# Value weighting ahead of the fill: the order of TensorE's work in 53 steps of an attention and feed-forward block

## What is computed

```python
# x: (1024, 256); 16 heads of 128; WINDOW = 128
h = layernorm(x)
q, k, v = split_heads(h @ wq), split_heads(h @ wk), split_heads(h @ wv)
q, k = rotary(q, cos, sin), rotary(k, cos, sin)
valid = (k_pos > q_pos - WINDOW) & (k_pos <= q_pos)
attn = softmax(where(valid, (q @ k.T) * scale, neg))
x = x + merge_heads(attn @ v) @ wo
# feed-forward, w1q and w2q rounded to -1, 0, 1 by their mean absolute value
x = x + gelu(layernorm(x) @ w1q.T + b1) @ w2q.T + b2
```

## Time and profile before

| | |
|---|---|
| median of 3 runs | 348.57 us (347.9 to 349.16) |
| the profiled execution | 347.75 us |
| its span, first to last instruction | 346.0 us |
| TensorE, matmuls | 336.5 us, 97% |
| TensorE, weight loads | 311.8 us, 90% |
| VectorE | 272.2 us, 79% |
| ScalarE | 207.7 us, 60% |
| GpSimd | 222.8 us, 64% |
| granted TensorE clock | 1.00 in every slice |

### The profile page before, as it was taken

The page is one execution under the profiler, slowest core; times in us unless marked ns, Lnnn a source line. Parts: engine busy times, 40 slices in busy tenths (PEclk is TensorE's granted clock), DMA queues, the critical chain, the costliest instruction groups (busy, mean ns, idle before and its releaser), DMA issues.

```text
span 346.0 us, 6907 instructions
## 1 busy us (share of the span) xinstructions
PE 336.5 (97%) x2398; PEld 311.8 (90%) x2398; DVE 272.2 (79%) x608; ACT 207.7 (60%) x628; POOL 222.8 (64%) x181
## 2 busy tenths in 40 slices
PE   7997999999999999999999999999999999989996
PEld 7886789999999999999999999999999999968986
DVE  5888987778777887688779998898778777878682
ACT  3355766655677677555675566556665666466280
POOL 3426896867676777667889798979767657230400
PEclk9999999999999999999999999999999999999999
DMA  6832553455553333333233333333322232000001
GB/s 212 208 97 69 146 153 93 121 149 156 133 146 99 83 79 91 94 92 93 70 87 83 83 76 94 91 94 93 91 63 61 56 83 48 0 3 0 32 30 61
DMA packets 29025, 31.25 MB, mean 90 GB/s; under 512 B 3392, under 2 KB 20288, under 8 KB 28992
## 3 DMA queue, kind: packets, MB, share of 16 engines
q1 hardware_dynamic: 28672, 30.29, 34.4%
q10 hardware_dynamic: 320, 0.52, 0.4%
HBM read 12.98 MB, written 1.05 MB: 41 GB/s over the span
## 4 chain that ended last, share of the span: by engine, by line
PE 84%; DVE 6%; POOL 4%; issue 2%; ACT 2%; DMA 1%; SPq 0%; DVEq 0%; POOLq 0%
PE PR L423 22%; PE OT L504 13%; PE VO L442 12%; PE VO L459 12%; PE SC L477 11%; PE PT L488 4%; PE PR L532 2%; PE VO L539 2%; PE SC L532 2%; POOL gT_lo L1084 1%; POOL turn L1079 1%; DMA v_raw<-in_wv 1%; PE SC L539 1%; DVE probsT L870 1%; DVE gT_lo L845 1%
## 5 line engine op out<-in xcount | busy, mean ns | idle before, releaser
L1084 POOL TENSOR_TENSOR gT_lo<-turn,gT_hi 128x512 fp32r<-128x512 f32 x61 | 80.4, 1317 | 42.9 <-ACT gT_hi L669 42.6
L1079 POOL TENSOR_TENSOR turn<-turn,swapped 128x512 f32<-128x512 f32 x61 | 78.9, 1294 | 27.8 <-DMA swapped<-by_sin 27.7
L674 ACT ACTIVATE probs<-SC,negmax 128x128 f32<-128x128 f32 x128 | 45.8, 363 | 73.6 <-DVE negmax L859 73.6
L870 DVE TENSOR_TENSOR probsT<-PT,mask_sb 128x512 f32<-128x512 f32 x64 | 44.1, 689 | 39.6 <-PE PT L488 39.6
L504 PE MATMUL OT<-probsT,v_sb 128*128 128x128 f32 x450 | 60.4, 276 | 1.4 <-DVE probsT L870 1.0
L504 PEld LDWEIGHTS OT<-probsT,v_sb 128*128 128x128 f32 x450 | 55.3, 191 | 2.7 <-DVE probsT L870 2.6
L681 ACT ACTIVATE probs<-probs,rinv 128x128 f32<-128x128 f32 x128 | 44.5, 394 | 16.6 <-DVE rinv L864 16.6
L423 PE MATMUL PR<-xT_hi,qk_lo 128*128 128x512 f32 x128 | 50.6, 395 | 0.2 <-DVE xT_lo L809 0.2
L423 PE MATMUL PR<-xT_hi,qk_hi 128*128 128x512 f32 x128 | 50.4, 394 | 0.0
L423 PE MATMUL PR<-xT_lo,qk_hi 128*128 128x512 f32 x128 | 50.3, 393 | 0.0
L669 ACT CAST gT_hi<-turn 128x512 fp32r<-128x512 f32 x64 | 38.9, 607 | 9.8 <-POOL turn L1079 7.6
(11 more groups left out here) (118 smaller groups left out, 838.9 us busy)
## 6 DMA issues: line engine op xcount, KB each, us to landing
swapped<-by_sin SPq DMA_DIRECT2D x124, 128.0 KB, 2.3
v_raw<-in_wv SPq DMA_DIRECT2D x8, 256.0 KB, 3.1
qk_raw<-in_wq SPq DMA_DIRECT2D x16, 128.0 KB, 2.5
qk_raw<-in_wk SPq DMA_DIRECT2D x16, 128.0 KB, 2.6
o_raw<-in_wo SPq DMA_DIRECT2D x8, 256.0 KB, 3.0
xres<-in_x SPq DMA_DIRECT2D x4, 256.0 KB, 4.0
w_raw<-in_w1t SPq DMA_DIRECT2D x4, 256.0 KB, 3.1
w_raw<-in_w2t SPq DMA_DIRECT2D x4, 256.0 KB, 3.2
```

The costliest lines, as they stand in the source:

```text
L674: nc.scalar.activation(probs[n % 2][:, i], SC[n % 2][:, i * 256 + P:(i + 1) * 256], ACT.Exp, bias=negmax[:, n % 2, i:i + 1], accum_out=row ...
L870: tt(probsT[:], PT[:, 0:256].rearrange("p (i q) -> p i q", i=2).unsqueeze(2).broadcast_to([P, 2, 2, P]), mask_sb[:].unsqueeze(1).broadcast ...
L1079: tt(turn[m % 4][:], turn[m % 4][:], swapped[m % 2][:], ALU.add).then_inc(rot_done, 1)
L1084: tt(rot_lo(head, c % 2)[:, half_of(c)], turn[m % 4][:], rot_hi(head, c % 2)[:, half_of(c)].bitcast(F32), ALU.subtract).then_inc(rotlo_don ...
```

## The change

In steps 8 to 60 TensorE's list has `weigh_v(n-1)` ahead of `fill(n)`. Everything else stays, the other engines' lists too; `transpose_probs(n)` stands at the head of the next step as before.

```diff
                 if n + 4 < CHUNKS:
                     project(n + 4)
-                fill(n)
-                if n == STEPS - 1:
-                    transpose_half(0)
-                weigh_v(n - 1)
+                if turned_first(n):
+                    weigh_v(n - 1)
+                    fill(n)
+                else:
+                    fill(n)
+                    if n == STEPS - 1:
+                        transpose_half(0)
+                    weigh_v(n - 1)
             ffn1(0)
```

## The result

The changed kernel takes 364.52 us (median, 364.37 to 365.03) against 348.31 us before: a ratio of 1.048, with a 95% interval of 1.045 to 1.051, and 16.2 us more. The forecast was 364.9 us. Its profiled execution has a span of 362.6 us where the one before had 346.0.

A forecast was written before the change was run, and what follows sets the result against it. TensorE, never waiting in steps 8 to 59, was taken as the bound. 11.3 + 1.4 + 4.2 = 16.9 us, less 0.6, made 16.3 and, from the 348.57 us median, 364.9 us; 8-in-10 range 359.5 to 368.5.

The forecast's parts named there:

- What bounds the kernel: Steps 8 to 59: TensorE never waits, its matmul rows cover 238.00 of 238.00 us; an added wait costs in full.
- The bank wait: Steps 8 to 59: the moved weighting waits for `ot_lo` to empty bank OT, 11.3 us in all, bounds 6.1 to 13.9.
- the two outliers: Two steps where `ot_lo` ends 0.41 and 0.38 us late behind ternary-weight work; longer steps may give back some 0.6 us.
- Rival 3: VectorE's late steps with ternary pieces reach TensorE, 2.8 us, and a handover of 0.20 adds 2.6: up to 370 us; chance 0.05.
- The second return to fp32r: Fill behind the fp32 weighting: one more change of operand type a step, 0.08 us each, 53 times, 4.2 us.
- The rival that had it free: At the fill behind the weighting, the return to fp32r costs nothing: 360.7 us; chance 0.08.
- the handover of 0.15: From the end of `ot_lo` to the weighting: a wait late by x costs x + 0.15 us, in 52 steps.
- Step 60: No projection there, so the weighting waits for `ot_lo` and the fill's hidden 1.42 us come behind: 1.4 us.
- What stays covered: Transposition's wait for `scaled` (0.63 us of cover), earlier `ot_hi`, later `copy_v` and `add_out`: no cost or gain.
- What would show it: Steps 8 to 59: some 50 OT weight-load waits of 0.1 to 0.3 us, fill spacing 0.20 then 0.12, steps of 4.9.

The follow-up runs named there:

- split fill: Changed kernel with, in steps 8 to 60, six fill products ahead of the weighting and six behind it: 348.81 us, 1.002 of the kernel before.
- run with one product ahead: Changed kernel with, in steps 8 to 60, one fill product ahead of the weighting and eleven behind it: 359.04 us, 1.032 of the kernel before.
- two products ahead: Changed kernel with, in steps 8 to 60, two fill products ahead of the weighting and the other ten behind: 352.41 us, 1.012 of the kernel before.

## Why the prediction came out

Its sum was right to 0.4 us, but two of its terms were wrong by some 3.7 us, one each way. That they cancelled was not foreseen: with either one put right alone the forecast would have missed by about 4 us.

- **What bounds the kernel: right.** TensorE had no slack in steps 8 to 59, so every wait added is paid in full. With the cover kept (split fill) it stays full, and nothing is lost.
- **The bank wait: right in place, too small in size.** The sum had 11.3 us less 0.6 for the two outliers. The outliers went, as forecast: in the changed kernel `ot_lo` ends 1.41 to 1.52 us behind the projection's first product in every step. Rival 3's late VectorE steps showed only in the run with one product ahead, once. The lateness of `ot_lo` was right too: 0.055 us a step on the mean, and 0.15 from its end to the first matmul make the 0.204 that the table shows. What was missing is 0.072 us in the weighting. The step that failed is the comparison "an unhindered weighting of eight takes 0.89 from start to start": that was read ahead of a transposition, while the hindered ones stood ahead of an fp32r product. Ahead of an fp32r product an unhindered weighting takes 0.82. So a late handover costs x + 0.22 us, and 52 x 0.276 = 14.4 us instead of 10.7.
- **The second return to fp32r: wrong.** It was priced at 4.2 us from a longer spacing. Runs with one and two returns more put it at 0.007 us a step, 0.4 us. The rival that had it free was right on this point, though its time of 360.7 was not, since it kept the handover of 0.15. A formula of the Trainium skill speaks to this, page "TensorE: Matmul & The Clock Gate", section "Back-to-back issue gap": it counts the columns alone. The section calls it the gap of an isolated matmul and says that in a stream the weight loads set the spacing too, which the prediction left out. The single rows at 0.20 us differ from the formula; the step's sum (4.560 against 4.553 us) agrees with it in having no price for what ran before.
- **The two errors are one.** The 0.07 us that a weighting seems to save ahead of an fp32r product and the 0.08 that this product seems to cost are the same overlap of rows, read once as a gain left out and once as a loss put in. That is why they are of one size.
- **Step 60: right.** 1.4 us forecast, 1.45 measured by itself.
- **What stays covered: right.** No wait of the transposition for `scaled`, of `copy_v` or of `add_out` turned up in the changed kernel, and the earlier `ot_hi` gave nothing, though ScalarE's waits for it (5.2 us) are gone.
- **What would show it: half right.** The waits are there, 52 of them, but they read 0.44 us on the mean, not 0.1 to 0.3, as they count from the end of the load before; and the profile names "issue", not the tile. Step 31, from which the 4.91 us were worked out, takes 4.88; the mean is 4.85, as 14 of the 52 weightings have six rows.

The runs give 14.4 + 0.4 + 1.4 = 16.2 us for the change. The medians differ by 16.2, the profiled spans by 16.6: 0.010 us a step, in the fill behind the weighting (1.509 against the split fill's 1.499), stay unexplained.

## What to carry to other kernels

On an engine without slack, work moved ahead of other work is safe only as far as what it waits for is done by then: compare the end of the releaser with the start of the place it moves to, step by step, and add about 0.2 us for the handover (0.22 here), since the weight load wants to be ahead of its matmul. Three small products ahead of the waiting one, 0.35 us, were enough here, while two left 0.05 us a step; splitting a filler gives freedom of order that moving it whole does not. Don't price a change of type or neighbour by the spacing of two rows alone: take the whole stretch from one group's start to the end of the next. And don't read a wait's cost from the idle time of matmul rows: of 15 us lost here they showed 2.

## What was not expected of the hardware

- An fp32 weighting takes 0.83 us from start to start ahead of a transposition and 0.75 ahead of an fp32r product (means over weightings of six and of eight rows), whose own first row is 0.36 us long instead of 0.28. The sum is the same to 0.01 us.
- A product of 256 columns behind one of 128 columns has the next start 0.17 us later instead of 0.12, with fp32r on both sides.
- A weight load that comes up to about 0.07 us late doesn't move the start of its matmuls, but the group takes that much longer (0.787 against 0.749 us with two products ahead): it ends 0.92 us behind the load's start for eight rows.
- Three returns from fp32 to fp32r in a step cost no more than one (4.559 and 4.553 us).
